# B's row in PSUM turned into dt*u*B in place and scanned from there, in a four-layer vision kernel

## What is computed

```
def step(h, t):
    dt_t, u_t, B_t, C_t = t
    h = h * jnp.exp(dt_t[..., None] * A) + (dt_t * u_t)[..., None] * B_t[:, :, None, :]
    y = jnp.einsum('bkdn,bkn->bkd', h, C_t)
    return (h, y)
```

## Time and profile before

| | us |
|---|---|
| three runs | 30998.21, 31024.93, 31036.17 |
| median | 31024.93 |
| span of the profiled execution | 31070.8 |
| busy: GpSimd | 23383.1 |
| busy: VectorE | 23050.6 |
| busy: TensorE | 23014.3 |
| busy: ScalarE | 12015.2 |

### The profile page before, as it was taken

The page is one execution under the profiler, slowest core; times in us unless marked ns, Lnnn a source line. Parts: engine busy times, 40 slices in busy tenths (PEclk is TensorE's granted clock), DMA queues, the critical chain, the costliest instruction groups (busy, mean ns, idle before and its releaser), DMA issues.

```text
span 31070.8 us, 287429 instructions
## 1 busy us (share of the span) xinstructions
PE 23014.3 (74%) x94224; PEld 14570.5 (47%) x94224; DVE 23050.6 (74%) x38816; ACT 12015.2 (39%) x20358; POOL 23383.1 (75%) x21172
## 2 busy tenths in 40 slices
PE   5578778787787778777877787777877787777444
PEld 4444445444544454444544454444544454435433
DVE  1289887888588868888788859886788858885212
ACT  1144444444344434443444434443444444433000
POOL 6777777777677777777777767777677777656767
PEclk7788889888888888888988889888888888888666
DMA  3212122221221221212222121212222121112221
GB/s 75 75 50 64 54 66 65 57 64 51 71 61 51 64 73 51 64 50 57 70 58 63 49 72 53 59 51 64 58 58 61 50 72 52 51 42 67 64 57 53
DMA packets 2410662, 1854.55 MB, mean 60 GB/s; under 512 B 1686546, under 2 KB 2045508, under 8 KB 2409164
## 3 DMA queue, kind: packets, MB, share of 16 engines
q0 software_dynamic: 677376, 1388.62, 16.1%
q1 hardware_dynamic: 1731788, 447.55, 6.5%
HBM read 1569.35 MB, written 265.21 MB: 59 GB/s over the span
## 4 chain that ended last, share of the span: by engine, by line
POOL 61%; issue 18%; PE 12%; DVE 6%; ACT 2%; DMA 1%; SPq 1%; DVEq 0%; POOLq 0%; ACTq 0%
POOL d_g L730 61%; PE d_p L1014 2%; PE d_pr L1162 2%; DVE l_wk L1311 1%; PE l_acc L996 1%; DVE l_wk L1288 1%; DVE d_g L1325 1%; PE d_pr L1049 1%; PE l_pc L1127 1%; DVE l_wk L1305 1%; PE d_pr L1216 1%; DMA d_xin<-mid 0%; SPq L629 0%; DVE l_wk L1290 0%; PE d_pr L1209 0%
## 5 line engine op out<-in xcount | busy, mean ns | idle before, releaser
L730 POOL DMA_INDIRECT d_g<-table,d_idx x21168 | 23382.9, 1105 | 7645.0 <-issue 6426.9
L1014 PE MATMUL d_p<-d_g,c_ident 128*128 128x128 f32 x43200 | 6292.8, 312 | 2702.1 <-DVE d_g L1325 2697.1
L1014 PEld LDWEIGHTS d_p<-d_g,c_ident 128*128 128x128 f32 x43200 | 6108.4, 226 | 3849.1 <-DVE d_g L1325 2820.6
L996 PE MATMUL l_acc<-l_wk,c_ident 128*128 128x448 f32 x14336 | 7295.8, 639 | 436.7 <-DVE l_yx L1276 348.4
L1325 DVE TENSOR_TENSOR d_g<-d_g,d_wt 128x512 f32<-128x512 f32 x5304 | 3361.9, 689 | 3335.2 <-DMA d_g<-table,d_idx 3333.1
L781 ACT ACTIVATE l_pm<-l_wk,l_a 128x448 f32<-128x448 f32 x3584 | 2272.9, 634 | 7292.9 <-DVE l_wk L1288 7287.8
L1301 DVE TENSOR_TENSOR l_wk<-l_wk,l_pb 128x896 f32<-128x896 f32 x3584 | 3824.5, 1067 | 1501.6 <-PE l_pb L965 1499.4
L996 PEld LDWEIGHTS l_acc<-l_wk,c_ident 128*128 128x128 f32 x14336 | 3176.0, 223 | 2507.2 <-issue 2334.0
L1311 DVE TENSOR_TENSOR l_wk<-l_wk,l_pc 128x896 f32<-128x896 f32 x3584 | 3808.2, 1063 | 25.3 <-ACT l_carry L762 21.1
L1288 DVE TENSOR_TENSOR_SCAN l_wk<-l_pm,l_carry,l_wk 128x448 f32<-128x448 f32 x3072 | 3505.4, 1141 | 4.2 <-ACT l_pm L781 1.6
L1305 DVE TENSOR_TENSOR_SCAN l_wk<-l_wk 128x224 f32<-128x224 f32 x3584 | 2432.1, 679 | 0.3
(11 more groups left out here) (178 smaller groups left out, 22691.0 us busy)
## 6 DMA issues: line engine op xcount, KB each, us to landing
d_g<-table,d_idx POOLq DMA_INDIRECT x21168
table<-d_pst SPq DMA_DIRECT2D x2376, 64.0 KB
hd<-d_hst SPq DMA_DIRECT2D x168, 224.0 KB
d_htc<-hd SPq DMA_DIRECT2D x144, 256.0 KB
d_xin<-mid SPq DMA_DIRECT2D x112, 224.0 KB
mid<-d_xo SPq DMA_DIRECT2D x192, 128.0 KB
d_xres<-mid SPq DMA_DIRECT2D x192, 128.0 KB, 2.2
d_xin<-in_x SPq DMA_DIRECT2D x56, 224.0 KB
```

The lines of the kernel that those rows point to most:

```text
L730: e.indirect_dma_start(out=m.g[Q % SLOTS][:, j, :], out_offset=None, in_=m.table[k % 2], in_offset=bass.IndirectOffsetOnAxis(ap=m.idx[G % ...
L996: ins = e.matmul(m.acc[:, h, 0:448], m.ident[:, :], m.hb[x % 4][:, h, :], start=(n == 0), stop=(n == 15))
L1014: ins = e.matmul(m.p0[:, t % 2 * 128:t % 2 * 128 + 32 * w], m.ident[:, :], m.g[Q % SLOTS][:, w * p:w * p + w, 32 * r:32 * r + 32], start=( ...
```

## The change

The product with B becomes two instructions of one half each: that of half 0 goes to `hb` as before, that of half 1 is written over B's row in the bank `l_pb`. The scan of half 1 is one instruction over all 448 pixels, which reads dt*u*B from `l_pb` and writes h to `hb`; it, and no longer the product, releases the bank (`f_pb`). A new semaphore `bm` counts the two products. On VectorE the order of the step is now scan 0, scan 1, product with C of step S - 1, the two products with B of step S + 1. The item `sB` is gone: B's row is issued inside `s`, behind C's row and ahead of the accumulation, and waits for the scan of half 1 of step S. ScalarE waits for the counters that the scans now give.

```diff
--- before.py
+++ after.py
@@ -79,7 +79,7 @@
                 out += [(0.5, [("c", i, c, h, part)]) for part in range(3)]
         out += [(0.3, [("h", i, 0, m)]) for m in range(9)]
         for sig in range(-1, NSTEP + 3):
-            tick = [("sB", i, sig - 1)] * (0 <= sig < NSTEP) + [("s", i, sig)]
+            tick = [("s", i, sig)]
             j, q = divmod(sig, 16)
             if 0 <= sig < NSTEP:
                 if 2 <= q <= 10 and j + 1 < len(PIECES):
@@ -367,12 +367,8 @@
     if kind == "s":
         _, i, sig = item
         s = NSTEP * i + sig
-        if sig == -1:
-            return [("pb", ("B", s + 1))]
-        return [("pc", ("C", s - 1))] if 1 <= sig <= NSTEP else []
-    if kind == "sB":
-        _, i, sig = item
-        return [("pb", ("B", NSTEP * i + sig + 2))] if sig + 2 < NSTEP else []
+        uses = [("pc", ("C", s - 1))] if 1 <= sig <= NSTEP else []
+        return uses + [("pb", ("B", s + 1))] if sig + 1 < NSTEP else uses
     if kind == "g":
         _, i, c, m = item
         q = 7 * i + c
@@ -758,7 +754,8 @@
                 kd, c = PIECES[(sig - 1) // 16]
                 n = (sig - 1) % 16
                 end = 0 if kd >= 2 else 447
-                e.wait_ge(s["sh"], 2 * S)
+                e.wait_ge(s["sh"], S)
+                e.wait_ge(s["f_pb"], J.free("B", S - 1))
                 e.activation(m.carry[:, :, n], m.hb[(S - 1) % 4][:, :, end], ACT.Copy).then_inc(s["ca"], 1)
             for q, h in ((0, 1), (1, 1), (0, 0)) if sig == -1 else ((sig + 2, 1), (sig + 1, 0)):
                 if q >= NSTEP or sig > NSTEP:
@@ -775,9 +772,9 @@
                 if h == 1 and q == 0 and i:
                     e.wait_ge(s["p_pc"], J.full("mo", 7 * i - 1))
                 if h == 0 and x:
-                    e.wait_ge(s["sh"], 2 * x - 1)
+                    e.wait_ge(s["sh"], x)
                 if h == 1 and x >= 3:
-                    e.wait_ge(s["sh"], 2 * x - 4)
+                    e.wait_ge(s["f_pb"], J.free("B", x - 3))
                 e.activation(m.dA0 if h == 0 else m.dA1[x % 3], m.dt[P % 2][:, h, :], ACT.Exp,
                              scale=m.aa[:, kd, h, n:n + 1]).then_inc(s[f"dA{h}"], 1)
         elif kind == "h":
@@ -978,12 +975,12 @@
         if kind == "s":
             _, i, sig = item
             S = NSTEP * i + sig
-            if sig == -1:
-                row_of_B(S + 1)
             if 1 <= sig <= NSTEP:
                 if J.use["C", S - 1]:
                     e.wait_ge(s["f_pc"], J.use["C", S - 1])
                 spread(S - 1, m.pc, 16).then_inc(s["p_pc"], 1)
+            if sig + 1 < NSTEP:
+                row_of_B(S + 1)
             if 2 <= sig <= NSTEP + 1:
                 x = S - 2
                 P, n = divmod(x, 16)
@@ -995,10 +992,6 @@
                 for h in range(2):
                     ins = e.matmul(m.acc[:, h, 0:448], m.ident[:, :], m.hb[x % 4][:, h, :], start=(n == 0), stop=(n == 15))
                 ins.then_inc(s["accd"], 1)
-        elif kind == "sB":
-            _, i, sig = item
-            if sig + 2 < NSTEP:
-                row_of_B(NSTEP * i + sig + 2)
         elif kind == "sum":
             _, k, t, u = item
             Q = NQ * k + 3 * t + u
@@ -1280,14 +1273,20 @@
                 hb, dA1 = m.hb[S % 4], m.dA1[S % 3]
                 ini = [0.0 if c == (6 if kd >= 2 else 0) else m.carry[:, h, n:n + 1] for h in range(2)]
 
-                way, one, two, mid = slice(None), slice(0, 224), slice(224, 448), 223
-                if kd >= 2:
-                    way, one, two, mid = slice(None, None, -1), slice(447, 223, -1), slice(223, None, -1), 224
-                e.wait_ge(s["f_pb"], J.free("B", S))
+                way = slice(None, None, -1) if kd >= 2 else slice(None)
+                row = m.pb[:, 0:448]
+                e.wait_ge(s["bm"], 2 * S + 1)
                 e.wait_ge(s["dA0"], S + 1)
                 e.tensor_tensor_scan(hb[:, 0, way], m.dA0[:, way], hb[:, 0, way], ini[0], ALU.mult, ALU.add).then_inc(s["sh"], 1)
+                e.wait_ge(s["bm"], 2 * S + 2)
                 e.wait_ge(s["dA1"], S + 1)
-                e.tensor_tensor_scan(hb[:, 1, one], dA1[:, one], hb[:, 1, one], ini[1], ALU.mult, ALU.add).then_inc(s["s1h"], 1)
+                e.tensor_tensor_scan(hb[:, 1, way], dA1[:, way], row[:, way], ini[1], ALU.mult, ALU.add).then_inc(s["f_pb"], 1)
+            if 1 <= sig <= NSTEP:
+                x = S - 1
+                e.wait_ge(s["p_pc"], J.full("C", x))
+                e.wait_ge(s["ca"], x + 1)
+                e.tensor_tensor(m.hb[x % 4][:, :, :], m.hb[x % 4][:, :, :], bc(m.pc[:, 0:448], 1, 2),
+                                ALU.mult).then_inc(s["f_pc"], 1)
             if sig + 1 < NSTEP:
                 x = S + 1
                 P, n = divmod(x, 16)
@@ -1298,18 +1297,8 @@
                     for b, v_ in enumerate(both(7 * i + 6)):
                         e.wait_ge(s[f"xn{b}"], v_)
                 e.wait_ge(s["p_pb"], J.full("B", x))
-                e.tensor_tensor(m.hb[x % 4][:, :, :], m.dtu[P % 2][:, :, :], bc(m.pb[:, 0:448], 1, 2),
-                                ALU.mult).then_inc(s["f_pb"], 1)
-            if 0 <= sig < NSTEP:
-                e.wait_ge(s["s1h"], S + 1)
-                e.tensor_tensor_scan(hb[:, 1, two], dA1[:, two], hb[:, 1, two], hb[:, 1, mid:mid + 1],
-                                     ALU.mult, ALU.add).then_inc(s["sh"], 1)
-            if 1 <= sig <= NSTEP:
-                x = S - 1
-                e.wait_ge(s["p_pc"], J.full("C", x))
-                e.wait_ge(s["ca"], x + 1)
-                e.tensor_tensor(m.hb[x % 4][:, :, :], m.hb[x % 4][:, :, :], bc(m.pc[:, 0:448], 1, 2),
-                                ALU.mult).then_inc(s["f_pc"], 1)
+                e.tensor_tensor(m.hb[x % 4][:, 0, :], m.dtu[P % 2][:, 0, :], m.pb[:, 0:448], ALU.mult).then_inc(s["bm"], 1)
+                e.tensor_tensor(m.pb[:, 0:448], m.dtu[P % 2][:, 1, :], m.pb[:, 0:448], ALU.mult).then_inc(s["bm"], 1)
         elif kind == "weigh":
             _, k, t, u = item
             Q = NQ * k + 3 * t + u
@@ -1592,7 +1581,7 @@
 PLAIN = ("c_w l_w da xi0 xi1 tab0 tab1 hdo dg htc xr0 xr1 xo0 xo1 vx0 vx1 xn0 xn1 z0 z1 vr0 vr1 vo0 vo1 "
          "p_r0 p_r1 p_pm p_pb p_pc f_r0 f_r1 f_pm f_pb f_pc f_a0 f_a1 pa aexp cst dv "
          "weighed accq ysa ytp yta idx wtr w0 pv py exd bst agg sqd x1r xor gbr dgr bsq bnr "
-         "dA0 dA1 s1h sh ca accd d1 d2 hd0 md m2 lo ab ex uu qq s1 ln pag psq xir brd lag lsq xmr gsq gt gb tg").split()
+         "dA0 dA1 bm sh ca accd d1 d2 hd0 md m2 lo ab ex uu qq s1 ln pag psq xir brd lag lsq xmr gsq gt gb tg").split()
 
 
 def program(nc, a, out, n_img=8, layers=(0, 1, 2, 3)):
```

## The result

The changed kernel takes 32,911.15 us (median of 4 runs, 32,896.04 to 32,950.24), the kernel before beside it 31,023.78 us (4 runs). The ratio is 1.061, 95% interval 1.0595 to 1.0625: slower by 1,887 us. In a second measurement it was 1.0607 (1.0589 to 1.0625). The forecast was 31,725, slower by 700, with a range up to 32,500. The direction was right; the loss is 2.7 times the one forecast, and lies above the range.

What follows compares the result with a forecast made beforehand. GpSimd's gathers were taken as the bound. The dense stretch became 2003 + 319 + 0 + 19 = 2341 us, +85, x 10.45 = +890, cut to +700: 31,725 us as median, range 30,300 to 32,500.

Steps and rivals of the forecast that it cites:

- VectorE's own work: VectorE's products and scans: split products and one full scan cost 0 net, bounds -70 to +470 us in all.
- GpSimd's holds: Gathers held by scan halves with two SBUF inputs: removing this frees GpSimd 0.31 us a step, 1,110 us; bounds 0 to 2,290.
- The lockstep: TensorE and VectorE: B's row waits for scan 1, so a step lasts as long as the longer engine's work; chance 0.52.
- All four signs named in advance: Profile: gathers near 1.05 us, slot waits over 1,500, C and B product waits over 2,500, dense gather waits near nothing.
- Its size, 319 us a stretch: VectorE's waits for TensorE in the dense stretch: 277 us in intervals with a sum plus 42 in others, where 178 were.
- The fifth off: Whole-kernel loss cut from +890 to +700 us, arguing low clock stretches TensorE's work and an engine standing less has less.
- the rival of the deeper loss: TensorE, pausing every step, falls to the lower clock for another tenth of the time: +970 us more, 32,700; chance 0.10.
- The smaller terms: VectorE's 56 us a stretch of gather waits vanish, and stretches without scan do not change.
- The gain arrives: TensorE's waits cost no more than today, VectorE loses its gather waits and is the bound: 30,440 us; chance 0.25.
- Only the holds: TensorE is hardly late, GpSimd with unheld gathers still sets the end: 29,915 us as a median; chance 0.05.
- Nothing to measure: Shorter gathers and TensorE's lateness cancel within 0.2% at 234 us of lateness in the stretch; chance 0.08.

Runs made afterwards that it cites:

- the release alone: Two kernels in the change's order with half 1's product in SBUF, differing only in whether scan or product releases B's bank: 32,947.43 against 30,930.79 us.
- the early release: Changed kernel with half 1's product written to and scanned from SBUF, B's bank released by that product: 30,930.79 us, 0.9967 of the kernel before.
- the late release: Changed kernel with half 1's product written to and scanned from SBUF, B's bank still released by the scan: 32,947.43 us, 1.0617 of the kernel before.

## Why the prediction was right or wrong

**VectorE's own work, 0.** Right. Its step: products 0.53 us apart as taken, the write into PSUM free (620 ns against 611), the full scan 1.06; 2002.66 us against 2003.43 in the stretch, -114 us in the whole.

**GpSimd's holds, -1,110 us for GpSimd.** Right for the scans, and half of the whole: GpSimd saved 2,114 us, near the upper bound of 2,290. The dense gather was foreseen at 1.05 us and is 1.018 (1594.7 / 1566). A count over all gathers of both traces shows where the rest comes from; as held I take those over 1.005 us, since a gather that nothing holds lasts 0.945. Before, 2,017 held gathers end 0.75 to 0.77 us behind the end of L1290 and 2,054 behind that of L1305, and they lose 515 and 630 us by it. That is 1,145 us, 0.32 us a step, where the term had 0.31. It was a good estimate of the product, not of its factors: 57% of the scan halves hold a gather, where it supposed 0.66 / 1.45 = 46%, and a hold costs 0.28 us in the mean, where it supposed 0.33. After the change no gather is held so behind L1280 or L1283.

The other 970 us come from gathers held by other VectorE instructions, which the term left as they were: behind the weighing they lose about 750 us where they lost 1,260, behind the rest 530 where they lost 980. Why these holds became less is open: GpSimd stands 11,602.1 us where it stood 7,645.0, which may be a reason, and no run tried it. With the one full scan back on SBUF inputs 2,607 gathers are held behind it and lose 1,409 us, 0.39 a step, of 1,670 us in all.

The Trainium skill (SBUF — State Buffer, Who interferes with whom) makes one SBUF input against two the dividing line for a GpSimd instruction that reads SBUF, and the runs agree with it for these gathers: 1,005 ns with half 1's row in PSUM, 1,083 in SBUF. It did not matter for the time, as said in advance.

**The lockstep.** Right, and shown by the release alone: 2,017 us. All four signs named in advance came: gathers near 1.05, slot waits over 1,500 us (3,866.2), the waits before the C and B products over 2,500 (4,472.8), and none for gathers in the dense stretch (0.3 us).

**Its size, 319 us a stretch: the step that failed.** It measured 442. The step took TensorE's work in an interval with a sum, 7.10 us, over from the trace of before, at the clock of before, and it is 7.51 us after the change. I worked out TensorE's busy time in the interval from one B row to the next, over both whole traces (3,576 intervals; TensorE's busy time in brackets):

| interval | forecast, us | before, us | after, us |
|---|---|---|---|
| with a sum (1,347) | 7.20 | 8.60 (7.09) | 7.65 (7.51) |
| without (2,229) | 6.50 | 5.27 (3.79) | 6.75 (3.87) |

After the change TensorE is busy for 7.51 of the 7.65 us of an interval with a sum: that is what the lockstep means. The forecast's 7.10 us of work is what the trace of before has, 7.09, and its 0.1 for the handoffs is near the 0.14 left. What it left out is that the same instructions take longer behind the pauses. The release alone shows it too: 7.01 us in the kernel with the early release, 7.52 in that with the late one, at mean granted clocks of 0.839 and 0.806. The accumulation has 709 ns where it had 639, and TensorE's busy time grew by 705 us in the whole. The other half of the miss is in the intervals without a sum, for whose uneven items I allowed 0.2 us on top of 6.30 and which needed 0.45. Together these are 0.45 us in 1,347 intervals and 0.25 in 2,229, some 610 and 560 us. The waits for the rows therefore grew by 2,950 us in the whole and not by (319 - 178) x 10.45 = 1,473.

**The fifth off, -190 us.** Wrong in its sign. I argued that an engine that stands less has less of the low clock. TensorE did not stand less: it waits for the bank in 2,066 of the 3,584 steps, 5,743.7 us in all, its time outside of matmuls grew from 8,057 to 9,195 us, and the granted clock fell from 0.838 to 0.807. This was the rival of the deeper loss. By its own working it is 93 us a stretch, 0.7 for each sum; measured are 0.42 us in an interval with a sum (7.09 to 7.51), and 82 us in the whole stretch (1773.64 to 1855.99), some 10 of them for its 45 more matmuls. I gave it 0.10 and cut the range short of it, as if the low clock were a separate misfortune. The early and the late release show that it comes with the wait. Without taking the fifth off, and with the deeper loss as part of the lockstep, my own numbers would have given 31,025 + 890 + 970, about 32,900. That this is so near is in part luck: 0.7 was too much for the low clock, 0.2 too little for the uneven items, and two smaller terms, below, were too small on the side of the gain.

**The smaller terms.** The wait for gathers gave back about 880 us where 585 were counted, since it vanished in every stretch with scans. The rest of the program gained 142, counted at nothing.

**The rivals.** *The gain arrives* needed a lateness under 234 us a stretch; the early release, which has it, measured 0.997, not the 0.981 of that rival: with the row back in SBUF the gathers are held again (1,097 ns), and GpSimd sets the end. *Only the holds* needed the freed GpSimd to be the end; it is 8% of the chain. *Nothing to measure* needed the two effects to be equal; the waits for the rows grew by 2,950 us, against about 880 less of waits for gathers.

## What to carry to other kernels

A buffer that saves a pass or a port may be one that another engine refills. Before writing a result over an input, list who fills that buffer next, what stands behind that instruction on its in-order queue, and compare the longest work on that engine between two handoffs, not its mean, with the time between them. When two engines are put in lockstep, the sum is over intervals of the longer of the two, and the engine that is made to pause came back at a lower granted clock here (0.70 behind 3.78 us of standing): count that with the wait, not as a rival to it. If a bank must be held, do the work that frees it first: exchanging two scans of the same cost gave back 70% of the loss.

## What the runs showed that I had not expected

VectorE's product of 128x448 into PSUM over its own input costs 620 ns where into SBUF it costs 613, and a scan from PSUM 1,118 ns where from SBUF it costs 1,125: the place of the row is worth nothing to VectorE itself. One wait moved TensorE's mean granted clock from 0.839 to 0.806. A gather held by a scan from SBUF ended 0.75 to 0.77 us behind the scan every time. And one chip differed by more than the change: the kernel before took 31,011.67 to 31,036.55 us in three measurements and 35,334.49 on that chip, where waits of up to 47.8 us before the C product end at something the trace does not name, and where the wait at the bank cost 3.5% instead of 6.5%. What stops the engines there is open.
